# Gate products on four TensorE tiles, one per chunk of dimensions, and a second product that adds the four parts

## The reference, cut to what matters

```python
logits = xf @ gate_w                       # (1024, 512) @ (512, 8)
scores = jax.nn.softmax(logits, axis=-1)
top_scores, top_idx = jax.lax.top_k(scores, TOP_K)
```

## Time and profile before

| | |
|---|---|
| median of three runs | 747.01 us (745.41 to 749.55) |
| profiled execution, its own time | 746.17 us |
| its span in the profile | 744.4 us |
| TensorE busy | 96% of the span |
| gate products, 64 records, first and last start | 568.0 and 596.3 us |
| their busy time | 7.7 us |
| TensorE's share of the chain that ended last | 85% |

### The profile page before, as it was taken

How to read it: one execution, slowest core, us unless ns; L and a number is a source line. 1 busy time by engine, 2 the same in 40 slices (tenths; PEclk the granted TensorE clock), 3 DMA queues, 4 the chain that set the end, 5 groups by cost and what they waited for, 6 DMA issues and landing times.

```text
span 744.4 us, 14155 instructions
## 1 busy us (share of the span) xinstructions
PE 715.5 (96%) x4910; PEld 593.7 (80%) x4910; DVE 492.6 (66%) x904; ACT 441.5 (59%) x958; POOL 238.4 (32%) x207
## 2 busy tenths in 40 slices
PE   4899999999999999999999999999999979999996
PEld 3677888888888888888888888788778857788875
DVE  6766776775766757756667676967467875755573
ACT  4655776675766757756757565564655435556560
POOL 1462211221211212121212142753840023555534
PEclk9999999999999999999999999999999999999999
DMA  9931121212121212112212304631115457655659
GB/s 302 105 129 42 44 87 44 85 42 85 42 85 42 85 42 81 46 55 72 84 43 82 103 2 151 206 118 51 58 35 195 137 172 249 108 103 109 112 73 337
DMA packets 59672, 75.21 MB, mean 101 GB/s; under 512 B 8784, under 2 KB 33360, under 8 KB 59632
## 3 DMA queue, kind: packets, MB, share of 16 engines
q1 hardware_dynamic: 52032, 58.16, 26.0%
q0 software_dynamic: 4720, 11.27, 8.3%
q10 hardware_dynamic: 2880, 5.24, 2.0%
HBM read 54.75 MB, written 19.92 MB: 100 GB/s over the span
## 4 chain that ended last, share of the span: by engine, by line
PE 85%; DVE 7%; DMA 3%; ACT 3%; issue 2%; SPq 0%; POOL 0%; DVEq 0%; POOLq 0%; ACTq 0%
PE pK L32 42%; PE pV L32 11%; PE pP L32 9%; PE pV L1643 5%; PE pT L1544 4%; PE pT L1735 4%; PE pS L1687 2%; PE pP L1717 2%; DMA fin<-total 1%; PE pT L1882 1%; PE pT L1524 1%; PE pS L1812 1%; DMA total<-big,idx 1%; PE pS L1905 1%; DVE bst L1001 1%
## 5 line engine op out<-in xcount | busy, mean ns | idle before, releaser
L32 PE MATMUL pK<-parts 128*128 128x512 f32 x744 | 187.7, 399 | 0.0
L540 POOL TENSOR_TENSOR parts<-big,parts 128x1024 fp32r<-128x1024 f32 x32 | 77.9, 2435 | 309.5 <-ACT parts L767 309.5
L32 PEld LDWEIGHTS pK<-parts 128*128 128x128 f32 x744 | 134.4, 188 | 27.0 <-issue 1.2
L1043 DVE TENSOR_TENSOR kn<-pK,head_rs 128x512 f32<-128x512 f32 x62 | 42.9, 692 | 58.1 <-ACT head_rs L681 58.1
L32 PE MATMUL pK<-w,lhs 128*128 x276 | 69.1, 399 | 1.0 <-issue 0.6
L32 PEld LDWEIGHTS pK<-w,lhs 128*128 128x128 f32 x276 | 50.3, 188 | 12.4 <-issue 2.8
L1464 DVE TENSOR_TENSOR w_p<-big,w_p 128x1024 fp32r<-128x1024 f32 x22 | 27.0, 1226 | 37.8 <-ACT w_p L958 37.8
L32 PE MATMUL pP<-pT,parts 128*128 128x256 f32 x384 | 51.8, 284 | 0.1
L615 POOL DMA_INDIRECT big<-x_rows,idx_x x23 | 26.7, 1162 | 73.6 <-DVE idx_x L1420 59.4
L1037 DVE TENSOR_REDUCE head_ss<-sq 128x8 f32<-128x512 f32 x62 | 42.5, 685 | 11.5 <-ACT sq L675 11.5
L675 ACT ACTIVATE sq<-pK 128x512 f32<-128x512 f32 x62 | 36.8, 594 | 21.5 <-PE pK L32 21.4
(11 more groups left out here) (331 smaller groups left out, 1528.9 us busy)
## 6 DMA issues: line engine op xcount, KB each, us to landing
big<-in_ctx_dram SPq DMA_DIRECT2D x32, 512.0 KB, 3.8
total<-zero SPq DMA_DIRECT2D x32, 256.0 KB, 4.0
w_raw<-in_L_ffn_w_dram SPq DMA_DIRECT2D x16, 512.0 KB, 5.8
big<-in_L_ffn_w_dram SPq DMA_DIRECT2D x8, 512.0 KB, 4.3
fin<-total SPq DMA_DIRECT2D x8, 512.0 KB, 8.1
x_rows<-big ACTq DMA_DIRECT2D x8, 256.0 KB, 2.1
total<-big ACTq DMA_DIRECT2D x8, 256.0 KB, 2.3
big<-in_x_dram SPq DMA_DIRECT2D x1, 1536.0 KB, 10.4
```

Source lines behind the costliest of these rows:

```text
L32: last = pe.matmul(out, lhs(a, c), rhs(b, c), start=start and c == first and n == 0, stop=stop and c == chunks - 1 and n == 2)
L540: nc.gpsimd.tensor_tensor(ctxN[:, u, LO], ctx_raw[:, u], ctxN[:, u, HI].bitcast(F32), ALU.subtract).then_inc(cn_lo, 1)
L1043: tt(heads(kn[:, t]), heads(pKV[t][:, :]), per_head(head_rs[:, t]), ALU.mult).then_inc(k_n, 1)
```

## The change

The gate weights are now held and the tokens streamed. The gate weights of each chunk (128 dimensions by 8 experts) are padded with zeros to 32 columns in a buffer gw_pad that GpSimd clears at the start; the four chunks go to four tiles of TensorE, 128 rows by 32 columns each, and write four separate parts: partitions 32c to 32c+7 of p_part hold the logits of chunk c, as experts by 128 tokens. ScalarE copies p_part from PSUM to a buffer g_rows (`gate_rows_copy`), and a second product (`gate_sum`) with g_rows as weights and eight columns of a selection matrix as the streamed side adds the four parts and turns the result back to tokens by experts. The buffer g_rows is single. The semaphore g_part now says that the parts are there, g_copy that the copy is made, and g_mm that the sum is.

```diff
-        gw_raw = sb("gw_raw", [P, C, E])
+        gw_pad = sb("gw_pad", [P, C, S])
+        gw_raw = gw_pad[:, :, 0:E]
...
+        g_rows = at("g_rows", [P, P], 155 * KB + 64 + 448)
...
+        p_part = pS[:, 1, P:2 * P]
...
             nc.gpsimd.memset(ident[:, :], 0.0).then_inc(ident_step, 1)
+            nc.gpsimd.memset(gw_pad[:, :, :], 0.0)
...
+            def gate_rows_copy(t):
+                act.wait_ge(g_part, t + 1)
+                if t >= 1:
+                    act.wait_ge(g_mm, t)
+                act.activation(g_rows[:, :], p_part, ACT.Copy).then_inc(g_copy, 1)
+
             for s in range(TILES + 2):
...
                     if t >= 2:
-                        act.wait_ge(g_mm, t - 1)
+                        act.wait_ge(g_part, t - 1)
                     ln_high(2 * TILES + t, x3T[:, t % 2])
+                    if t >= 1:
+                        gate_rows_copy(t - 1)
                     act.wait_ge(ln_x, 2 * TILES + t + 1)
...
+            gate_rows_copy(TILES - 1)
             for g in range(2):
...
-                    nc.vector.tensor_reduce(sel[:, :], ident[:, 0:3 * B].rearrange("p (j b) -> p b j", j=3), AX.X, ALU.add).then_inc(sel_set, 1)
+                    nc.vector.tensor_reduce(sel[:, :], ident[:, :].rearrange("p (j b) -> p b j", b=B), AX.X, ALU.add).then_inc(sel_set, 1)
...
             def gate_product(t):
...
+                if t >= 1:
+                    pe.wait_ge(g_copy, t)
+                pe.nop(nofuse=True)
                 for c in range(C):
-                    last = pe.matmul(p_gate[t // HALF][:, t % HALF, :], x3T[:, t % 2, c, :], gw_raw[:, c, :], start=c == 0, stop=c == C - 1)
-                last.then_inc(g_mm, 1)
+                    last = pe.matmul(p_part[c * S:(c + 1) * S, :], gw_pad[:, c, :], x3T[:, t % 2, c, :], start=True, stop=True,
+                                     tile_position=(0, c * S))
+                last.then_inc(g_part, 1)
+
+            def gate_sum(t):
+                pe.wait_ge(g_copy, t + 1)
+                pe.matmul(p_gate[t // HALF][:, t % HALF, :], g_rows[:, :], sel[:, 0:E], start=True, stop=True).then_inc(g_mm, 1)
...
+                if t >= 1:
+                    gate_sum(t - 1)
                 if t >= 0:
                     gate_product(t)
+            gate_sum(TILES - 1)
```

More of the change, by code:

```diff
@@ L289, in perceiver_block @@
         g_mm, g_step, g_act, g_diff, gate_set = (sem(n) for n in ("g_mm", "g_step", "g_act", "g_diff", "gate_set"))
+        g_part, g_copy = sem("g_part"), sem("g_copy")
         zeroed, route_set, route_step = (sem(n) for n in ("zeroed", "route_set", "route_step"))
```

## The result

The changed kernel takes 748.93 us in the median of 13 runs (747.26 to 752.71), the kernel before 746.05 us in 13 runs of the same comparison (745.41 to 749.55). The ratio is 1.0032 with a 95% interval of 1.0020 to 1.0044: about 2.4 us slower, inside the half per cent that the forecast called "within". The profiled execution took 748.93 us with a span of 747.2 us.

What follows compares the result with a forecast made beforehand. TensorE bounds until turn 7, then choosing the experts on VectorE: 0.56 us VectorE lateness, 0.44 DMA issues, 0.26 copy, 0.52 sum and hand-overs give +1.8 us, median 748.8 us; range 746.0 to 750.9 us.

Steps and rivals of the forecast that it cites:

- within: Outcome class: measured time within about 0.5% (3.7 us) of no change; given 85%.
- The slots: TensorE gate slots: tiled product 0.38 us, sum 0.20 us, against 0.81 us for the old slot.
- G: TensorE's lead on reaching the gate slot of turn 7: 0.43 + 0.69 = 1.12 us.
- choose(0): VectorE waits 1.68 us for the sum of tile 3, starting 0.56 us late; TensorE then waits some 1.7 us.
- The last tile: Copy behind two DMA issues, then a sum, before choose(1): 0.44 + 0.26 + 0.52 us besides VectorE's 0.56 us lateness.
- Serial tiles: Rival: the four column tiles run one after the other, product 1.04 us, total +4.4, 751.4 us; chance 7%.
- Covered waits: Rival: VectorE and ScalarE waits are covered, TensorE stays the bound, total -0.8, 746.2 us; chance 7%.
- The full swap: Rival: a gate slot falls to a quarter, 0.20 us, and the sums hide; 4.9 us gained, 742.1 us; chance 3%.
- The clock: Rival: added pauses move the clock's fall, so low clock lasts through the 17 fillers; +4.6, 751.6 us; chance 6%.
- the priced case: The clock rival's case: 17 fillers from 605.26 at low clock take 3.65 us more, 2.9 us of it on top.
- the two slow rivals: Tiles one after the other (751.4 us, chance 7%) and the clock falling elsewhere (751.6 us, chance 6%).
- slower: Outcome class: slower by over 0.5%, through serial tiles, the clock or the very edge of the forecast's range; 12%.

Runs made afterwards that it cites:

- e4: The change with the copies of tiles 0 to 4 and sums of tiles 0 to 3 one projection earlier; 746.67 us, ratio 1.0022 to the kernel before.
- e3: The change with six filler products in TensorE's pause of turn 8, ahead of the sum of tile 4; 747.96 us, ratio 1.0035 to the kernel before.
- e8: e3 with the last copy moved ahead of the two DMAs of tile 7 on ScalarE; 746.79 us, ratio 1.0021 to the kernel before.
- e5: e4 with the last copy moved ahead of the two DMAs of tile 7 on ScalarE; 745.87 us, ratio 1.0000 to the kernel before.
- e2: The change with only tile 7 back to one product on the whole array; 747.67 us, ratio 1.0028 to the kernel before.
- e6: e4 and e2 together: early copies and sums, tile 7 in the old form; 744.46 us, ratio 0.9993 to the kernel before.

## Why the prediction was right, step by step

The forecast was 748.8 us, +1.8 on the median of three known then; measured are 748.93 us and a ratio that means +2.4 us (1.5 to 3.3). That the two times agree within 0.13 us is luck: the median of three from which the forecast started lies 1.0 us above the median of 13, and the loss was forecast 0.6 us too small by the ratio, 1.1 us by the medians. The waits appeared in the trace in their places, but the last copy was held by another engine than forecast, and two sizes were off, in the same direction.

**The slots.** Product 0.38 forecast, 0.36 measured, plus 0.09 where it follows the transposes; sum 0.20 forecast, 0.21 measured. The four tiles do run side by side: the eight records took 0.36 us, one after the other they would take 0.88 at 0.11 us each. TensorE reaches the gate slot of turn 7 at 27.13 us from the mark (587.59 - 560.46) where it was 28.11 (587.90 - 559.79): G is 0.98 where 1.12 was forecast. Turn 3 makes half of the difference, 0.81 - 0.45 = 0.36 in place of 0.43; turns 4 to 6 make the other half, 0.62 in place of 0.69.

**choose(0).** Forecast 0.56 us late, VectorE idle 1.68 us, TensorE idle some 1.7 in turn 8. Measured 0.71 late, idle 1.62 and 1.50. The difference of 0.15 us is the smaller G. The pause of TensorE is shorter than forecast because the forecast left out the first half of the counting, 0.22 us between projection and transposes (591.03 to 591.25). e4 shows the late choose(0) as a cause: with the sum of tile 3 earlier, both pauses are gone and choose(1) comes 1.76 us earlier, 0.47 of which is the clock (the part that e3 gave back).

**The last tile.** Forecast 1.22 us. In the changed kernel it is 2.66 - 0.71 = 1.95 us. This is the term that was mis-sized. With the clock at full (e3) it is 2.19 - 0.74 = 1.45 us, and the path is the forecast's: the DMA issues cost 0.62 us (e3 to e8) where 0.44 was forecast, the copy and the sum 1.57 - 0.71 = 0.86 us (e8) where 0.78 was. The 0.44 took the start of row_tok behind the DMAs as the start of the copy, 0.58 us after the second issue began; in e3 the copy started 0.83 us after it. In the changed kernel itself the path was another: at half clock the products and sums of tiles 6 and 7 took so long that the last copy waited for the product of tile 7, and the DMA issues ahead of it held nothing. The forecast had no term for that.

**The rivals.** Serial tiles: excluded by the slot of 0.36 us. Covered waits: excluded by the two pauses. The full swap: the slot came near half, not a quarter, and none of it reached the end. The clock: half right. It was priced only for the 17 fillers behind choose(1), which ran at full clock (608.66 to 612.79), but it did fall earlier, behind the pause of turn 8, and made the chain of tiles 6 and 7 slower by 0.47 us in the trace. "Fillers ran there" had been true of the kernel before and was not true of this one. The profiled execution of e5 shows a part of the priced case: its clock was at 0.50 from 606 to 608 us, and the 17 fillers took 5.72 us instead of 4.10, 1.62 us more where 3.65 was priced:

```profile
604.94 5.72 PE L1844 MATMUL pK<-w 128*128 128x512 f32 x17
...
618.17 0.66 PE L1913 MATMUL pT<-ident,big 128*128 128x128 f32 x4 [0.98 <-DMA big<-x_rows,idx_x]
```

That execution had a span of 746.7 us, though its choose(1) was only 0.15 us later than before the change; the median of its kernel is 745.87 us. How often an execution goes this way, no run here counts. The chances do not add up by one point: the two slow rivals alone have 13%, where the forecast gives 12% to slower.

**What stays open.** How much of the 2.4 us the half clock makes: 0.47 us by two traces, nothing that the timed medians of e3 could show. Nor was a second p_part and g_rows tried, with the product of tile 7 ahead of the sum of tile 6; whether that undoes the chain of tiles 6 and 7 is not shown.

## What to carry to other kernels

A cheaper operation that hands its result through another engine moves the result to a later place in the program: ask who waits for it there, and what is queued behind the waiter, before counting the microseconds saved. Here the slots saved 1.0 us by turn 7, and a wait of VectorE, queued ahead of the statistics of the next tile, took that and more; moving the sum one projection earlier, and leaving the old form where its result is needed at once, turned +2.4 into -1.3 us. At the end of a loop, count the position behind DMA issues on the same engine as a cost, about 0.6 us in the traces here, but only where the operation would otherwise be ready: at half clock it was not. And check whether a new pause of TensorE has work under it that a lower clock would slow.

## What the runs showed of the hardware that was not expected

In the changed kernel the granted clock fell to 0.50 behind a pause of TensorE of 1.50 us, with short gate products and transposes around it; in e3, with six fillers in that pause, it stayed at 1.00 until past 599 us. In e2, which keeps the pause of turn 8 without fillers, it fell between 593 and 594 us. The other traces show it fall between 596 and 600 us, around the pause of 2.54 us before the counting.

The instruction of ScalarE behind the two DMA issues started 0.83 and 0.88 us after the start of the second issue in e3 and e4, where it is the copy, and 0.58 us after it in the kernel before, where it is row_tok. The instruction alone does not decide this: in e2 and e6 it is row_tok again, and it started 0.78 and 0.80 us after the issue. What makes the difference is not shown.
